# One pass loop written out 26 times becomes a hardware loop, and the gather indices come through a small buffer

## The reference, cut to what matters

```python
# layer 0, twice: gather, add an edge term, segment MAX
msg = x[src] @ W_msg + edge_attr @ W_edge
agg = segment_max(msg, dst);  x' = leaky_relu(agg + x @ W_root + b)
# layer 1: gather, multiply with an edge network, segment SUM
w   = relu(edge_attr17 @ W1.T + b1) @ W2.T + b2
agg = segment_sum(w * x[src], dst);  relu(x @ Ws.T + bs + agg @ Wn.T + bn)
# layer 2: two hops of a normalised adjacency; layer 3: one hop, then a product with a weight
h = segment_sum(norm[:, None] * h[src], dst)
```

## Time and profile before

| | |
|---|---|
| three runs, median | 5191.91 us (5186.35 to 5204.22) |
| the profiled execution | 5186.35 us, span 5184.5 us |
| granted TensorE clock, mean | 0.775 |
| busy share PE / DVE / ACT / POOL | 79% / 44% / 19% / 50% |
| gathers of `gath`, POOL | 2496, 965 ns each |
| the three edge passes with their node parts | about 4,290 us of the span |
| the dense part | about 895 us |

### The profile page before, as it was taken

One profiled execution on the slowest core, in us unless ns is written; L12 is line 12 of the kernel. 1 busy time (PEld: TensorE's weight loads), 2 busy tenths in 40 slices (PEclk: granted clock), 3 DMA queues, 4 the chain that ended last, 5 costly groups with the idle time before them and its releaser, 6 DMA issues.

```text
span 5184.5 us, 56871 instructions
## 1 busy us (share of the span) xinstructions
PE 4090.3 (79%) x19316; PEld 2666.9 (51%) x19316; DVE 2258.3 (44%) x5877; ACT 1004.6 (19%) x2108; POOL 2585.1 (50%) x2689
## 2 busy tenths in 40 slices
PE   5676767677267777877774899899988869999999
PEld 4333333333233333333333455555555549999999
DVE  3454545455134545454543455455555552223211
ACT  1000000000122222222223233333333340001101
POOL 4566666665556666666655555555555540000000
PEclk9999999999966656555655655555566669999999
DMA  4333333333134444444432333333433427777776
GB/s 128 94 101 90 100 92 99 95 96 92 45 84 130 127 131 127 132 127 131 126 108 62 101 115 117 117 115 117 118 113 116 117 95 260 265 269 268 263 260 219
DMA packets 261995, 695.05 MB, mean 134 GB/s; under 512 B 83518, under 2 KB 166142, under 8 KB 237950
## 3 DMA queue, kind: packets, MB, share of 16 engines
q1 hardware_dynamic: 66626, 348.21, 19.8%
q0 software_dynamic: 85568, 131.83, 12.7%
q10 hardware_dynamic: 109564, 212.08, 11.0%
HBM read 477.81 MB, written 214.09 MB: 133 GB/s over the span
## 4 chain that ended last, share of the span: by engine, by line
PE 52%; another core or an unknown queue 24%; DVE 14%; issue 6%; ACT 3%; DMA 1%; POOL 0%; DVEq 0%; ACTq 0%; POOLq 0%
PE banks L1096 17%; PE banks L960 7%; PE banks L1001 6%; PE banks L936 5%; DVE scan L1809 5%; PE banks L956 5%; PE banks L927 5%; PE banks L974 4%; DVE hot_lo L1462 3%; DVE hot_key L1826 2%; DVE hot_hi L1464 1%; DVE hot_src L1828 1%; PE banks L715 1%; ACT adj L1329 1%
## 5 line engine op out<-in xcount | busy, mean ns | idle before, releaser
L689 POOL DMA_INDIRECT gath<-table,ids x2496 | 2407.6, 965 | 1493.2 <-issue 752.2
L1809 DVE TENSOR_TENSOR_SCAN scan<-keep,scan,banks 96x512 f32<-96x512 bf16 x621 | 791.2, 1274 | 1776.8 <-remote 1143.4
L974 PEld LDWEIGHTS banks<-ident,scan 96*128 96x128 f32 x2496 | 401.1, 223 | 972.3 <-DVE scan L1809 525.5
L1096 PE MATMUL banks<-r_parts,adj_in 128*128 128x288 bf16 x7203 | 891.5, 287 | 4.8 <-DVE r_parts L1510 2.9
L1096 PEld LDWEIGHTS banks<-r_parts,adj_in 128*128 128x128 bf16 x7203 | 883.6, 142 | 7.9 <-DVE r_parts L1510 3.6
L974 PE MATMUL banks<-ident,scan 96*128 96x96 f32 x2496 | 532.0, 361 | 371.0 <-DVE scan L1809 346.1
L960 PE MATMUL banks<-ea,w_edge 32*96 32x512 f32 x832 | 781.4, 1032 | 19.4 <-issue 17.8
L1001 PE MATMUL banks<-hot_key,hot_src 128*128 128x392 bf16 x1600 | 559.7, 486 | 236.1 <-issue 144.9
L1311 ACT ACTIVATE back<-banks 128x384 f32<-128x384 f32 x624 | 305.8, 490 | 2191.2 <-remote 1090.0
L1826 DVE TENSOR_SCALAR hot_key<-iota_key,key_t 128x392 bf16<-128x392 int16 x1600 | 533.5, 333 | 20.9 <-ACT key_t L1350 20.9
L936 PEld LDWEIGHTS banks<-w_edge_out,hid 97*128 97x128 f32 x1664 | 316.4, 284 | 323.1 <-issue 323.0
(11 more groups left out here) (158 smaller groups left out, 2110.1 us busy)
## 6 DMA issues: line engine op xcount, KB each, us to landing
adj_in<-adjacency SPq DMA_DIRECT2D x147, 1568.0 KB
scanned_rows<-back ACTq DMA_DIRECT2D x153, 768.0 KB
adjacency<-adj ACTq DMA_DIRECT2D x100, 784.0 KB
ea<-in_ea_t SPq DMA_DIRECT2D x156, 256.0 KB
gath<-table,ids POOLq DMA_INDIRECT x2496
keep<-keep_max_d SPq DMA_DIRECT2D x104, 384.0 KB
keep<-keep_sum_d SPq DMA_DIRECT2D x52, 384.0 KB
table<-x_sb SPq DMA_DIRECT2D x10, 240.0 KB, 4.4
```

What stands on the lines that cost most here:

```text
L689: pool.indirect_dma_start(gath[:, b, t, :], None, tables[p][:, :], bass.IndirectOffsetOnAxis(ap=ids[:, 1, n:n + 1], axis=0),).then_inc(s_g ...
L974: m = pe.transpose(back_ps[g8 % 2][:, t * D:(t + 1) * D], scan[0:D, b, Q * g + t:Q * (g + 1):QT], ident[0:D, 0:D])
L1096: m = pe.matmul(sum_ps[:, u, j, :], adj_in[:, a, :, h], r_parts[:, n % 2, h, :, :].rearrange("p k f -> p (k f)"), start=h == 0, stop=h == ...
L1809: ve.tensor_tensor_scan(scan[0:D, b, at:at + Q], keep[:, b, at:at + Q], turn_ps[k % 2], start, keep_op, take_op).then_inc(s_scan, 1)
```

## The change

`all_pairs` goes away. In the branch that is taken, SP, POOL, PE, ACT and DVE run their pairs through `over_pairs`, and `over_groups` gets an engine and runs as a loop too: four steps written out, three iterations of two steps, then the rest. Inside such a loop the pair number is a register, so wait values and addresses that depend on it are computed by register instructions (`REGISTER_ALU`, `ISA` in the listings below).

POOL no longer reads row numbers from the table `ids` at a fixed column. SP loads the 16 columns of a chunk from memory into `src_ix[:, b, :]` (128 partitions of 64 bytes), ahead of that chunk's `ea` and `keep`, once the 16 gathers that used the buffer last have landed; POOL waits for this transfer (`s_ix[b]`) at each chunk.

```diff
-        def all_pairs(pair, after_first=None):
-            for i in range(PAIRS):
-                pair(i, i == 0, i == PAIRS - 1)
-                if i == 0 and after_first:
-                    after_first()
-        def over_groups(*stages):
-            def step(i, b):
+        def over_groups(eng, *stages):
+            def step(i, b, known):
                 for stage, lag in stages:
-                    g = 2 * i + b - lag
-                    if 0 <= g < GROUPS:
-                        stage(g // 2, g % 2, g < 2)
-            for s in range(GROUPS + max(lag for _, lag in stages)):
-                step(s // 2, s % 2)
+                    g = 2 * i + b - lag if known else None
+                    if not known or 0 <= g < GROUPS:
+                        stage(i + (b - lag) // 2, (b - lag) % 2, known and g < 2)
+            for s in range(4):
+                step(s // 2, s % 2, True)
+            with eng.Fori(2, GPAIRS) as i:
+                step(i, 0, False)
+                step(i, 1, False)
+            for s in range(GROUPS, GROUPS + max(lag for _, lag in stages)):
+                step(s // 2, s % 2, True)
...
@@ SP, loads_of_pair
+                            tiles = bass.ds(CT * (2 * i + b), CT)
+                            if not first:
+                                for k in range(4):
+                                    sp.wait_ge(s_gath[4 * b + k], 16 * QT * (PAIRS * p + i))
+                                sp.sem_inc(s_passed, 1)
+                            sp.dma_start(src_ix[:, b, :], src_t[:, tiles]).then_inc(s_ix[b], 16)
...
-                    all_pairs(loads_of_pair)
+                    over_pairs(sp, loads_of_pair)
...
@@ POOL, gather_pair
-                pool.wait_ge(s_ids, 32)
...
+                            pool.wait_ge(s_ix[b], 16 * (PAIRS * p + i + 1))
...
-                                    n = CT * (2 * i + b) + t
...
-                                        bass.IndirectOffsetOnAxis(ap=ids[:, 1, n:n + 1], axis=0),
+                                        bass.IndirectOffsetOnAxis(ap=src_ix[:, b, t:t + 1], axis=0),
...
-                    all_pairs(gather_pair)
+                    over_pairs(pool, gather_pair)
...
@@ PE, ACT, DVE: the same call
-                    all_pairs(pair, turn_lines if p == 0 else None)
+                    over_pairs(pe, pair, turn_lines if p == 0 else None)
-                    all_pairs(pair, leave_lines if p == 0 else None)
+                    over_pairs(act, pair, leave_lines if p == 0 else None)
-                    all_pairs(pair, make_keys if p == 0 else None)
+                    over_pairs(ve, pair, make_keys if p == 0 else None)
```

More of the change, by code:

```diff
@@ L467, in nodes @@
                 if p == 0:
-                    over_groups((store_y(n, tables_v[1]), 0))
+                    over_groups(sp, (store_y(n, tables_v[1]), 0))
                 elif p == 1:
@@ L472, in store_node @@
                         sp.dma_start(of_group(tables_v[2], i, b), node[:, b, :, :]).then_inc(s_table[n][b], 16)
-                    over_groups((store_node, 0))
+                    over_groups(sp, (store_node, 0))
                 elif p < 5:
@@ L477, in store_r @@
                         sp.dma_start(of_group(tables_v[p + 1], i, b), of_group(r_sb, i, b)).then_inc(s_table[n][b], 16)
-                    over_groups((store_r, 0))
+                    over_groups(sp, (store_r, 0))
                 else:
-                    over_groups((store_y(n, out_v), 0))
+                    over_groups(sp, (store_y(n, out_v), 0))
             is_general = sp.value_load(general[0:1, 0:1], min_val=0, max_val=1)
@@ L634, in gather_ends @@
                         ).then_inc(s_agg[n][b], 16)
-                over_groups((gather_ends, 0))
+                over_groups(pool, (gather_ends, 0))
             is_general = pool.value_load(general[0:1, 0:1], min_val=0, max_val=1)
@@ L785, in nodes @@
                 if stages:
-                    over_groups(*stages)
+                    over_groups(pe, *stages)
             is_general = pe.value_load(general[0:1, 0:1], min_val=0, max_val=1)
@@ L1204, in nodes @@
                 if stages:
-                    over_groups(*stages)
+                    over_groups(act, *stages)
             is_general = act.value_load(general[0:1, 0:1], min_val=0, max_val=1)
@@ L1324, in take_windows @@
                             n = WINDOWS * tile + 2 * k + j
-                            if k % 4 == 0 and j == 0 and not (p == 1 and under(i, 0, 1)):
+                            if k % 4 == 0 and j == 0 and not (p == 1 and type(i) is int):
                                 act.wait_ge(s_adj[half], 16 * tile)
@@ L1612, in nodes @@
                         ve.wait_ge(s_adj[half], 16 * 2 * BUILT)
-                over_groups((end_ix_ahead, 0), *{0: [(add_and_rectify, 0)],
+                over_groups(ve, (end_ix_ahead, 0), *{0: [(add_and_rectify, 0)],
                                   1: [(add_and_rectify, 0), (factors, 0)],
```

## The result

| | before | changed | ratio of fast runs, 95% interval |
|---|---|---|---|
| the measured pair | 5198.07 us (4 runs) | 5490.2 us (5473.93 to 5496.11, 4 runs) | 1.0559 [1.0525, 1.0592] |
| profiled execution, span | 5184.5 us | 5476.3 us | +291.8 us |

A forecast was written before the change was run, and what follows sets the result against it. POOL's gathers plus one pause per chunk were taken to bound pass 0, TensorE pass 2. 5186.35 + 45 + 13 + 0 + 8 + 0 = 5252 us, 5258 against the runs' median (+1.3%); range 5160 to 5345.

The forecast's parts named there:

- A: Pass 0: index load lands 0.9 us late behind the `keep` load in 50 chunks, +45 us (0 to 55).
- B: Pass 1: the same index wait, late in only 15 of 50 chunks at 0.9 us, +13 us (0 to 45).
- C: Pass 2: the index wait falls into POOL's 313.5 us of pauses for `msg_now`, 0 us; upper end +90.
- D: Passes 1 and 2: register instructions ahead of VectorE's one-hot operations, 0.09 us each, mostly hidden; +8 us (0 to 70).
- E: Loop ends: 72 rounds of compare, branch and new number per engine, 0.31 us each on TensorE; 0 us (0 to 22).
- F: Whole program: shorter code, fewer instruction loads, and the removed wait for the table of row numbers; gain 0.
- Rival 1: Passes 0 and 1: the index wait only shortens the later pause or the load lands early; about 5197 us, chance 0.24.
- Rival 2: Passes 0 and 1: the small pause releases TensorE's results, so the long pause shrinks; 5150 us, chance 0.20.
- Rival 3: Loop ends: each jump back refetches instructions, 151 to 216 us over 72 rounds; 5343 to 5408 us, chance 0.08.
- theory B: Pass 2, added during the experiments: 16 gathers without a pause hold up other engines' finished work; +200 us or more.

The follow-up runs named there:

- k1: The changed kernel again, unaltered, in a round where the kernel before took 4426.87 us: 4429.2 us, ratio 1.0002 to the kernel before.
- h2: The changed kernel with the index load issued a chunk earlier, all loops kept; 5189.6 us, 1.0135 of the kernel before (5122.24 us).
- h1: The changed kernel again, unaltered, in a round where the kernel before took 5122.24 us: 5490.45 us, ratio 1.072 to the kernel before.

## Why the prediction was wrong, step by step

- **What bounds the kernel** (gathers at 1.25 us plus one pause a chunk, ended in bursts): right for pass 0 under the late condition, from whose trace it was read. It is not a property of the kernel, as I took it: in the prompt rounds the pause is missing. That TensorE sets the period of pass 2 was wrong too: k1 does the same pass at 20.5 us a chunk instead of 26.2, with TensorE busy 1043 of 1065 us where it was busy 1187 of 1361.
- **A, the index wait in pass 0**: forecast +45 us, measured +40; the period was forecast at 24.5 us and is 1270 / 52 = 24.4. The number came, the mechanism did not, so the hit is in part luck. I had written of an idle time of about 1.2 us at most chunks and "the long pause unchanged". Instead the long pause moved to the chunk's start. In the middle of the pass 17 of these pauses are ended by the index load, 92.6 / 17 = 5.4 us each, and the "remote" waits fell from 38 of 3.6 us to 31 of 2.3 us.
- **B, pass 1**: forecast +13 us (0 to 45), measured +45, the upper end of its range. The count was about right and the size was not: 19 of 50 chunks wait for the index load (I took 15), but for 74.5 / 19 = 3.9 us each, not 0.9, and 39 chunks start with a pause where 13 did before.
- **C, pass 2: this step failed.** I took 0 with the words that "the wait falls into the 313.5 us of pauses". A pause is cover only for a wait that runs beside it. The index load is released by the scan, which stands right behind the message that used to end the pause. Its chain of scan, `keep`, issue and landing (1.19 + 0.23 + 0.68 + 3.48 us) begins when the pause would have ended, and most of it is added: +204 us, where even the upper end was 90. The upper end took twice the 0.9 us per chunk of pass 0, where the load's lead was 4 us; in pass 2 its lead was nothing.
- **D, register instructions**: forecast 0.09 us more between VectorE's one-hot operations and 8 us in all. The 0.09 us are not there. From the first of four pairs to the message behind them it is 3716.74 - 3715.19 = 1.55 us before and 3835.49 - 3833.94 = 1.55 us after, and in pass 2 the medians of both pitches are the same in the two traces (0.23 and 0.16 us). What the earlier trace rows show for one kind of operation did not carry over to another. POOL's pitch stays 1.25 us as well, as I took it.
- **E, jumps back**: forecast 0 us. In the prompt rounds the loops alone make 0.9997 to 0.9998 of the time, and the whole change 1.0002. Under the late condition h2 holds D, E and the early index load together to 67 us. Against the trace of before, its passes 1 and 2 are 9 and 6 us longer.
- **F, instruction loads**: they fell from 1.98 to 0.54 MB in the queue of the earlier trace rows, with no gain seen. In pass 2 from 3000 to 4300 there is one packet in each instruction queue, while TensorE jumps back 21 times at 32 + 207 + 50 ns (columns as in the earlier trace rows):

```profile
q8 instruction: 1, 0.02, 0.0%
q14 instruction: 1, 0.01, 0.0%
```

```profile
L383 PEldq ALU_OP  x21: 32/32/32, 3036.1 to 4254.5; - x21
L383 PEldq COMPARE_BRANCH  x21: 207/207/208, 3036.2 to 4254.6; - x21
L383 PEldq FUSED_REGOPS  x21: 50/50/55, 3036.5 to 4254.8; - x21
```

- **Rival 1** (the pauses only move) describes half of what happened: they moved, but grew longer. **Rival 2** (the small pause helps) did not come: no pass is shorter. **Rival 3** (each jump back stalls) is refuted by these rows: 21 jumps, two instruction packets. The rule of the Trainium skill, page "Runtime: NRT & Kernel Launch", section "Instruction fetch mechanics", that a branch out of the held pages forces a fetch, is not contradicted. These loops seem to stay within what is held, which is an inference from the two packets.

Between the profiled executions 66 us were forecast and 292 measured. C missed by 204 us and B by 32, A and D were 5 and 8 us too high, and 3 us lie outside the passes: 204 + 32 - 5 - 8 + 3 = 226.

What is shown: that the place of the index load in SP's order makes 301 of the 368 us under the late condition (h1, h2), and that the cost needs that condition (k1). What is read from traces but not tried under it: the chain's share of 4.9 us per chunk, and theory B. What stays open: the last 67 us, whether the index load costs the same without any loop, and what the late condition is.

No version beat the kernel before under either condition.

## What to carry to other kernels

Before a wait is called hidden in a pause, find what ends the pause and what starts the new wait; if the second hangs on the first, or on something just behind it, its latency is added, here 204 of an estimated 235 us, however long the pause is. A small load that feeds the engine which paces the kernel belongs ahead of the large loads and their waits in its queue, a whole buffer's turn early. And a bound read from one trace may be that of the condition it was taken under: here the same program took 4430 or 5190 us, and the change cost 0.0% or 5.5 to 7.2%. So measure a variant and its yardstick side by side, and look at the yardstick's own time first.

## What the runs showed of the hardware that I had not expected

- Two conditions. The scan (1.27 us) and a gather (0.95 us) take the same time in both. But under the late one the hand-over from TensorE to ScalarE took more than 1 us in 95 of 192 cases of pass 0 (up to 9.3 us) of the kernel before, and under the prompt one 0.04 us in all 192 of k1. The whole kernel differs by 16 to 17%.
- Where no gather ran, the hand-over was not late: behind the last gather of each pass it took 0.04 to 0.12 us under the late condition too.
- The number of a chip did not tell the condition: number 1 was prompt in one round and late in another. It was only seen by running the kernel before beside each variant.
- An 8 KB load of row numbers (128 pieces of 64 bytes), issued 0.68 us behind a load of 384 KB in the same queue, took 3.48 us (medians of pass 2) from its issue to the gather that waited for it.
- A register instruction ahead of each of VectorE's one-hot operations added nothing to them: four pairs take 1.55 us with it and without.
